# Six-layer local transformer inside a larger block: squares kept in the buffer of the rotated queries and keys, ten places instead of eight for split weight pieces, and the next layer's pieces split at other steps

## The chip, the cores and the metric

The kernel runs on one core of a Trainium2 chip. Its time is the device time of one execution in microseconds (us); lower is better. TensorE is called PE, VectorE DVE, ScalarE ACT, GpSimd POOL, and SyncE, which here issues all transfers, SP.

## The reference

The whole program is two blocks with adaptive layer norm. The first block's second half is a local transformer of six layers over 2 x 1024 tokens of width 128. The change touches only that part. One of its attention layers computes:

```python
qkv = x @ Wqkv                       # x shifted by one token in its upper 64 features
q, k, v = split into 16 heads of 64
q = l2norm(q) * qs
k = l2norm(k) * ksc
q = q * cos * scale + rotate_half(q) * sin * scale
k = k * cos * inv + rotate_half(k) * sin * inv
out = local_attention(q, k, v)       # windows of 32 tokens, each sees itself and the one before
out = out @ Wo
```

`l2norm` divides each head of a token by the root of its sum of squares. After attention and a residual comes a feed-forward part with layer norm and an exact gelu gate, and a second residual. Weights differ from layer to layer.

## The kernel before

`local_transformer` cuts the 2 x 1024 tokens of a layer into 16 slots of 128 tokens, so six layers are 96 slots. One software pipeline runs over all of them: a loop over steps, written out once per engine, in which step i works on several slots at once. In step i, PE projects queries and keys for slot i+2 (`project_qk`, four matrices of 512 columns), turns slot i's rotated queries and keys around (L803), computes slot i's scores (L824), projects the values of slot i+1 (`project_v`, two pieces), weighs the values of slot i-1 (L853) and projects slot i-2 out (L875). Every second step also takes a share of the feed-forward part: `up` and the gates fall into odd steps, `down` into even ones. Each engine works through its own list in the written order, so what stands at a place of the list waits for all that stands ahead of it.

**Weight pieces.** A layer's query, key and value matrix of 3072 columns is cut into six pieces of 512. The kernel multiplies in two parts, so each piece is split: SP loads it into `w_raw` (two buffers in turn, L580), ACT rounds it into `w_high` (L947), and POOL takes the difference into `w_low` (L696). `w_high` and `w_low` have `WS` places, and piece k of the whole run (k = 6 * layer + j) lies in place k % WS. Pieces j = 0 to 3 are queries and keys, 4 and 5 the values. Before a place is filled again, `wait_place` waits for the last matrix product that read it. With eight places, pieces 0 and 1 of a layer find a free place well ahead, while pieces 2 to 5 lie where pieces 0 to 3 of the running layer lie, and can be split only after that layer's last projection from them, in step -3. I write step -k for the step that stands k ahead of the first slot of the next layer, thus step 16 * layer - k. A layer has 16 slots, so step -k is an even step where k is even. There are five such layer boundaries. The first projection from a new query or key piece is in step -2, from a new value piece in step -1.

**When a piece is loaded and split** is set by two tables of step numbers: one in `splits_at`, which ACT and POOL both go by, and one in SP's loop. ACT splits j < 4 in the middle of its step and j >= 4 at the end of it. POOL splits j < 4 between the two halves of a slot's rotation, and j >= 4 one step later: the first of them ahead of the rotation, a second between its halves.

**One slot's norm and rotation.** ACT copies the projections into `qk` (L954) and squares them into `sq` (L960). DVE sums the squares by head (L1076) and takes the larger of that and 1e-24 (L1078, a tiny instruction with two inputs in SBUF). ACT takes logarithm and exponential (L966, L968). DVE scales `qk` by it (L1084, the first instruction of DVE's step), then multiplies with the cosines into `qr` (L1091). POOL multiplies the swapped halves with the sines into `t_sin` (L728, two per half slot) and adds them into `qr` (L733). Every second step POOL also stages the next inputs (L703, L705) and scales the next tables (L715), in odd steps. DVE's residual add (L1131, `h_mid`) and its product for the gate (L1150, `lt_f_gate`) empty banks of PSUM that PE's next products wait for: four banks go round in a ring.

Of the kernel before, what the change touches and what calls it, by code (L numbers as in the profile page):

```python
# [9 lines left out]
ALU = mybir.AluOpType  # L10
ACT = mybir.ActivationFunctionType
AX = mybir.AxisListType

P = 128
# [9 lines left out]
HD = 64  # L24
# [5 lines left out]
INNER = HEADS * HD  # L30
# [361 lines left out]
def local_transformer(nc, A, sb, sem, bank, ident, mean_w, eps, h_in, h_mid, padded):  # L392
# [3 lines left out]
    CHUNKS = ALL // 2  # L396
    BLOCKS = SLOTS // 2
    WCH = 6
    WS = 8
    with ExitStack() as ctx:  # L400
        def buf(name, shape, dt=F32):
            return sb(f"lt_{name}", shape, dt, ctx=ctx)

        w_high = buf("w_high", [P, WS, CH], F32R)
        w_low = buf("w_low", [P, WS, CH], F32R)
        w_raw = buf("w_raw", [P, 2, CH])
# [11 lines left out]
        x_high = buf("x_high", [P, 2, B, BLK], F32R)  # L418
        x_low = buf("x_low", [P, 2, B, BLK], F32R)
        qk = buf("qk", [P, 2, 2 * INNER])  # L420
        sq = buf("sq", [P, 2 * INNER])
        ssq = buf("ssq", [P, 2, 2 * HEADS])
        rn = buf("rn", [P, 2, 2 * HEADS])
        least = buf("least", [P, 2 * HEADS])
        t_sin = buf("t_sin", [P, INNER])
        qr = buf("qr", [P, 2, 2 * INNER])
        q_t = buf("q_t", [P, 2, PAIRS, BLK])
        k_t = buf("k_t", [P, 2, PAIRS, WIN + BLK])
# [25 lines left out]
        S = type("S", (), {n: sem(f"s_lt_{n}") for n in names})  # L454
# [13 lines left out]
        def live(g):  # L468
            return 0 <= g < ALL

        def even(i, back):
            c = (i - back) // 2
            return c if (i - back) % 2 == 0 and 0 <= c < CHUNKS else None
# [11 lines left out]
        def has_look(g):  # L485
            return g % SLOTS >= 2


        def splits_at(i):
            ks = []  # L490
            for layer in range(1, LAYERS):
                for j, at in enumerate((-8, -7, -3, -3, -2, -2)):
                    if i == SLOTS * layer + at:
                        ks.append(WCH * layer + j)
            return ks

        def wait_place(eng, k):

            if k >= WS:
                layer, j = (k - WS) // WCH, (k - WS) % WCH  # L500
                g = SLOTS * layer + SLOTS - 1
# [71 lines left out]
        with nc.Block(no_gpsimd_drain=True) as blk:  # L573
            @blk.sync
            def _(sp):
                def load_w(k):
                    if k >= 2:
                        sp.wait_ge(S.w_low, k - 1)
                    layer, j = k // WCH, k % WCH
                    sp.dma_start(w_raw[:, k % 2, :], A["lt_wqkv"][layer][:, j * CH:(j + 1) * CH]).then_inc(s_w[k % 2], 16)  # L580
# [9 lines left out]
                def load_scale(layer, i):  # L590

                    r = layer % 2
                    if i == 0 and layer >= 2:
                        sp.wait_ge(S.tab_scaled, BLOCKS * (layer - 1))
                    src = A["lt_qkscale"][layer]
                    if i == 0:
                        sp.dma_start(qk_scale[:, r, 0, :], src.to_broadcast([P, 2 * HD])).then_inc(s_scale[r], 16)
                    else:
                        a, h = (i - 1) // 2, (i - 1) % 2
                        to, at = HD * a + 32 * h, HD * a + 32 - 32 * h  # L600
                        sp.dma_start(qk_scale[:, r, 1, to:to + 32], src[:, at:at + 32].to_broadcast([P, 32]))\
                          .then_inc(s_scale[r], 16)

                def load_x(c):
                    if c >= BLOCKS:
                        sp.wait_ge(S.ff_out, c - BLOCKS + 1)
                    if c >= 2:
                        sp.wait_ge(S.staged, c - 1)
                    for f, back in halves:
                        sp.dma_start(x_s[f, c % 2, :, :], block(h_in, c, back, f)).then_inc(s_x[c % 2], 16)  # L610

                def load_v(g):
                    sp.wait_ge(S.v_out, 2 * (g + 1))
                    if g >= 2:
                        sp.wait_ge(S.av, g - 1)
                    if has_look(g):
                        for par in range(2):
                            lo = HD * par
                            sp.dma_start(v[lo:lo + WIN, g % 2, 0, :, :], v[lo + WIN:lo + 2 * WIN, g % 2, WPB - 1, :, :])\
                              .then_inc(S.look, 16)  # L620
                    for par in range(2):
                        lo = HD * par
                        src = v_tok[:, g % 2, par, :].rearrange("p (h d) -> p h d", d=HD)
                        sp.dma_start(v[lo + WIN:lo + 2 * WIN, g % 2, 0, :, :], src[0:WIN]).then_inc(s_v[g % 2], 16)
                        for w in range(1, WPB - 1):
                            sp.dma_start(v[lo:lo + 2 * WIN, g % 2, w, :, :], src[WIN * (w - 1):WIN * (w + 1)])\
                              .then_inc(s_v[g % 2], 16)
                    if has_look(g):
                        sp.wait_ge(S.look, looks(g))
                    for par in range(2):  # L630
                        lo, w = HD * par, WPB - 1
                        src = v_tok[:, g % 2, par, :].rearrange("p (h d) -> p h d", d=HD)
                        sp.dma_start(v[lo:lo + 2 * WIN, g % 2, w, :, :], src[WIN * (w - 1):WIN * (w + 1)])\
                          .then_inc(s_v[g % 2], 16)

                def look_back(g):
                    sp.wait_ge(S.scores, g - 1)
                    sp.dma_start(k_t[:, g % 2, :, 0:WIN], k_t[:, g % 2, :, BLK:BLK + WIN]).then_inc(s_klook[g % 2], 16)

                def load_f_x(c):  # L640
                    sp.wait_ge(S.out_done, 2 * (c + 1))
                    if c >= 1:
                        sp.wait_ge(S.f_mean, c)
                    for f, back in halves:
                        sp.dma_start(f_x[f, :, :], block(h_mid, c, back, f)).then_inc(S.f_x, 16)
# [13 lines left out]
                    load_layer(0, n)  # L659
                for i in STEPS:  # L660
                    for layer in range(1, LAYERS):
                        for j, at in enumerate((-10, -9, -7, -6, -2, -2)):
                            if i == SLOTS * layer + at:
                                load_w(WCH * layer + j)
                    if even(i, -5) is not None and even(i, -5) >= 2:
                        load_x(even(i, -5))
                    if live(i + 1):
                        load_v(i + 1)
                    if live(i + 2) and has_look(i + 2):
                        look_back(i + 2)  # L670
                    if even(i, 3) is not None:
                        load_f_x(even(i, 3))

                    for layer in range(1, LAYERS):
                        n = i - (SLOTS * layer - 11)
                        if 0 <= n < 5:
                            load_scale(layer, n)
                        elif 5 <= n < 9:
                            load_layer(layer, n - 5)
# [13 lines left out]
            def _(pool):  # L693
                def split_low(k):
                    pool.wait_ge(S.w_high, k + 1)
                    pool.tensor_tensor(w_low[:, k % WS, :], w_raw[:, k % 2, :], w_high[:, k % WS, :].bitcast(F32),  # L696
                                       ALU.subtract).then_inc(S.w_low, 1)
# [81 lines left out]
            def _(pe):  # L779
                def project(g, use, k):  # L780
# [4 lines left out]
                    xh, xl = x_high[:, g // 2 % 2, g % 2, :], x_low[:, g // 2 % 2, g % 2, :]  # L785
                    pe.matmul(o, xh, w_high[:, k % WS, :], start=True, stop=False)  # L786
                    pe.matmul(o, xh, w_low[:, k % WS, :], start=False, stop=False)  # L787
# [155 lines left out]
            def _(act):  # L943
# [11 lines left out]

                def square_qk(g):
                    act.wait_ge(S.proj_out, 4 * (g + 1))
                    if g >= 1:
                        act.wait_ge(S.sumsq, g)
                    act.activation(sq[:, :], qk[:, g % 2, :], ACT.Square).then_inc(S.squared, 1)  # L960

                def invert_norms(g):
                    act.wait_ge(S.clamped, g + 1)
# [70 lines left out]
                for i in STEPS:  # L1034
# [8 lines left out]
                    for k in splits_at(i):  # L1043
                        if k % WCH < 4:
                            split_high(k)
# [24 lines left out]
            def _(dve):  # L1070
                def sum_squares(g):
                    dve.wait_ge(S.squared, g + 1)
                    if g >= 2:
                        dve.wait_ge(S.ln, g - 1)
                    q = ssq[:, g % 2, :]
                    dve.tensor_reduce(q, sq[:, :].rearrange("p (h d) -> p h d", d=HD), AX.X, ALU.add).then_inc(S.sumsq, 1)  # L1076
                    dve.wait_ge(S.sumsq, g + 1)
                    dve.tensor_tensor(q, q, least[:, :], ALU.max).then_inc(S.clamped, 1)  # L1078

# [1005 lines left out]
```

## Time and profile before

| what | value |
|---|---|
| median of 3 runs | 2867.06 us |
| lowest, highest | 2858.47, 2876.53 us |
| profiled execution, its own time | 2873.17 us |
| profiled execution, span from first to last instruction | 2871.4 us |
| mean granted PE clock in it | 0.958 |

The profiled execution lies 1.8 us above its own span, and 6 us above the median, inside the spread of the runs. The local transformer is the stretch from about 115 us to about 1830 us of the span. In the profile, "idle before" is the time in which an engine sat still ahead of an instruction, with the instruction that released it. The length of a step is read here from the start of one L1084 on DVE to the start of the next one.

### The profile page before, as it was taken

What the parts mean: (1) busy time and instruction counts of PE and PEld (TensorE: products, weight loads), DVE (VectorE), ACT (ScalarE), POOL (GpSimd) and SP (SyncE); (2) the same over time, 40 slices, a digit from 0 to 9 for tenths busy, and PEclk for the clock granted to TensorE, in tenths of its full rate; (3) what the DMA queues carried; (4) which work ended last, traced back from release to release, by engine and by line L of the source; (5) the groups of instructions that cost most, each with busy time, mean ns of one, the idle gap of its engine ahead of it and who ended that gap; (6) DMA issues with size and microseconds to landing.
All of it is one profiled execution on the core that took longest, in us unless ns stands there. A gap on an engine that the chain in (4) does not pass through costs nothing. (4 is left out here: it accounts for less than half of the span.)

```text
span 2871.4 us, 119349 instructions
## 1 busy us (share of the span) xinstructions
PE 2518.8 (88%) x52916; PEld 2039.6 (71%) x53012; DVE 2187.8 (76%) x2553; ACT 1879.1 (65%) x3665; POOL 1475.6 (51%) x1015
## 2 busy tenths in 40 slices
PE   5469989999999899989999999679999899986998
PEld 2257777777877787777777887457776677765887
DVE  5378888888888888888888887388888888983112
ACT  2357777777777777777777777466666666653443
POOL 0188887788778787877887776011221212211000
PEclk8689999999999999999999999889999999997999
DMA  0223433333343333433342333022232231210000
GB/s 32 60 66 90 99 89 75 84 92 85 76 99 93 82 77 91 98 79 84 89 102 68 79 90 71 16 64 60 46 69 54 52 69 41 63 33 16 15 22 30
DMA packets 274599, 193.97 MB, mean 68 GB/s; under 512 B 117544, under 2 KB 215856, under 8 KB 273968
## 3 DMA queue, kind: packets, MB, share of 16 engines
q1 hardware_dynamic: 274096, 186.49, 27.2%
q8 instruction: 411, 6.73, 1.0%
q14 instruction: 92, 0.75, 0.1%
HBM read 29.10 MB, written 1.05 MB: 10 GB/s over the span
## 5 line engine op out<-in xcount | busy, mean ns | idle before, releaser
L728 POOL TENSOR_TENSOR lt_t_sin<-lt_qk,lt_tab 128x512 f32<-128x512 f32 x384 | 685.3, 1806 | 298.4 <-DVE lt_qk L1084 294.8
L733 POOL TENSOR_TENSOR lt_qr<-lt_qr,lt_t_sin 128x1024 f32<-128x1024 f32 x192 | 454.9, 2369 | 29.3 <-POOL lt_t_sin L728 2.6
L1622 DVE TENSOR_REDUCE fa_neg_max<-bank 128x1 f32<-128x1024 f32 x256 | 301.1, 1217 | 91.1 <-PE bank L1449 90.6
L786 PE MATMUL bank<-lt_w_high,lt_x_high 128*128 128x512 f32 x576 | 283.8, 493 | 71.4 <-POOL lt_w_low L696 50.7
L1562 ACT ACTIVATE fa_prob<-bank,fa_neg_max 128x1024 f32<-128x1024 f32 x128 | 142.5, 1114 | 244.3 <-DVE fa_neg_max L1622 127.6
L1632 DVE STREAM_TRANSPOSE fa_prob_t<-fa_prob 128x1024 f32<-128x1024 f32 x256 | 301.8, 1217 | 0.0
L1472 PE MATMUL bank<-fa_prob_t,fa_v 32*64 32x128 f32 x16384 | 278.8, 276 | 20.0 <-issue 14.7
L1472 PEld LDWEIGHTS bank<-fa_prob_t,fa_v 32*64 32x64 f32 x16384 | 242.9, 131 | 67.1 <-issue 38.7
L1076 DVE TENSOR_REDUCE lt_ssq<-lt_sq 128x32 f32<-128x2048 f32 x96 | 219.1, 2282 | 80.5 <-ACT lt_sq L960 80.2
L803 PE MATMUL bank<-ident,lt_qr 128*128 128x128 f32 x1536 | 234.5, 276 | 32.7 <-POOL lt_qr L733 16.0
L974 ACT COPY lt_v_tok<-bank 128x512 f32<-128x512 f32 x192 | 112.4, 586 | 222.0 <-PE bank L788 222.0
L1380 POOL TENSOR_TENSOR fa_qk_low<-fa_raw,fa_qk_high 128x256 fp32r<-128x256 f32 x128 | 90.0, 729 | 317.3 <-ACT fa_qk_high L1552 317.0
L803 PEld LDWEIGHTS bank<-ident,lt_qr 128*128 128x128 f32 x1536 | 187.1, 142 | 82.4 <-issue 26.6
L954 ACT COPY lt_qk<-bank 128x512 f32<-128x512 f32 x384 | 231.4, 604 | 16.5 <-POOL lt_t_sin L728 4.8
L1084 DVE TENSOR_TENSOR lt_qk<-lt_qk,lt_rn 128x2048 f32<-128x2048 f32 x96 | 228.7, 2382 | 8.9 <-ACT lt_rn L968 8.9
L1091 DVE TENSOR_TENSOR lt_qr<-lt_qk,lt_tab 128x2048 f32<-128x2048 f32 x96 | 230.0, 2396 | 3.3
L787 PE MATMUL bank<-lt_w_low,lt_x_high 128*128 128x512 f32 x576 | 231.6, 402 | 0.7 <-issue 0.7
L788 PE MATMUL bank<-lt_w_high,lt_x_low 128*128 128x512 f32 x576 | 232.1, 403 | 0.0
L875 PEld LDWEIGHTS bank<-lt_prob_t,lt_w_o 128*128 128x128 f32 x1536 | 186.8, 192 | 11.5 <-issue 4.7
L853 PEld LDWEIGHTS bank<-lt_v,lt_prob_t 64*32 64x32 f32 x12288 | 131.2, 107 | 85.1 <-ACT lt_prob_t L995 65.1
L875 PE MATMUL bank<-lt_prob_t,lt_w_o 128*128 128x128 f32 x1536 | 188.3, 275 | 3.6 <-issue 3.6
L853 PE MATMUL bank<-lt_v,lt_prob_t 64*32 64x64 f32 x12288 | 151.6, 229 | 38.8 <-ACT lt_prob_t L995 22.0
(225 smaller groups left out, 5825.7 us busy)
## 6 DMA issues: line engine op xcount, KB each, us to landing
lt_v<-lt_v_tok SPq DMA_DIRECT2D x576, 128.0 KB, 2.4
fa_v<-fa_v_tok SPq DMA_DIRECT2D x256, 128.0 KB
lt_v<-lt_v_tok SPq DMA_DIRECT2D x192, 64.0 KB, 2.1
lt_k_t<-lt_k_t SPq DMA_DIRECT2D x84, 128.0 KB, 2.7
lt_v<-lt_v SPq DMA_DIRECT2D x168, 64.0 KB, 2.0
lt_w_raw<-in_lt_wqkv_dram SPq DMA_DIRECT2D x36, 256.0 KB, 3.9
lt_x_s<-h_in SPq DMA_DIRECT2D x96, 64.0 KB, 2.7
lt_f_x<-h_mid SPq DMA_DIRECT2D x96, 64.0 KB, 2.2
```

The costliest lines, as they stand in the source:

```text
L728: pool.tensor_tensor(dst[:, :, i, :], src[:, :, 1 - i, :], tab[:, g // 2 % 2, 1, at:at + 32].unsqueeze(1).to_broadcast([P, HEADS, 32]), AL ...
L733: pool.tensor_tensor(qr[:, g % 2, half], qr[:, g % 2, half], t_sin[:, :], ALU.add).then_inc(S.rotated, 1)
L786: pe.matmul(o, xh, w_high[:, k % WS, :], start=True, stop=False)
L787: pe.matmul(o, xh, w_low[:, k % WS, :], start=False, stop=False)
L788: return pe.matmul(o, xl, w_high[:, k % WS, :], start=False, stop=True)
L803: mm = pe.transpose(bank[:, turn_bank("turn", g, j), n * P:(n + 1) * P], qr[:, g % 2, (4 * j + n) * P:(4 * j + n + 1) * P], ident[:, :])
L853: mm = pe.matmul(bank[WIN * w:WIN * w + WIN, value_bank(g, par), hp * HD:(hp + 1) * HD], prob_t[f, g % 2, hp, WIN * w:WIN * w + WIN], v[f, ...
L875: mm = pe.matmul(o, w_o[:, layer % 2, hp, :], att_t[:, g % 2, hp, :], start=hp == 0, stop=hp == PAIRS - 1)
L954: act.copy(qk[:, g % 2, j * CH:(j + 1) * CH], bank[:, turn_bank("qk", g, j), :]).then_inc(S.proj_out, 1)
L1472: mm = pe.matmul(bank[d, 4 + a, 0:P].rearrange("p (u r) -> p u r", u=UPQ), v[rows, half % 2, kb, d], prob_t[rows, q % 2, par, :, 32 * kb:3 ...
L1622: dve.tensor_reduce(neg_max[:, u % 2, par:par + 1], bank[:, 2 * par:2 * par + 2, :].rearrange("p a n -> p (a n)"), AX.X, ALU.max, negate=T ...
L1632: dve.transpose(prob_t[:, q % 2, par, u % UPQ, :], prob[:, u % 2, par, :]).then_inc(S.turned, 1)
```

## The change

It does three things: ACT's squares go into the half of `qr` that the same slot's rotated values will take later, and `sq` is gone; with the space, `w_high` and `w_low` get ten places; and both tables of steps are new.

```diff
-    WS = 8
+    WS = 10
...
-        sq = buf("sq", [P, 2 * INNER])
...
         def splits_at(i):
...
-                for j, at in enumerate((-8, -7, -3, -3, -2, -2)):
+                for j, at in enumerate((-10, -8, -6, -4, -3, -2)):
...
-                        for j, at in enumerate((-10, -9, -7, -6, -2, -2)):
+                        for j, at in enumerate((-13, -12, -9, -7, -5, -3)):
                             if i == SLOTS * layer + at:
                                 load_w(WCH * layer + j)
...
                 def square_qk(g):
                     act.wait_ge(S.proj_out, 4 * (g + 1))
-                    if g >= 1:
-                        act.wait_ge(S.sumsq, g)
-                    act.activation(sq[:, :], qk[:, g % 2, :], ACT.Square).then_inc(S.squared, 1)
+                    if g >= 2:
+                        act.wait_ge(S.turned, 4 * (g - 1))
+                    act.activation(qr[:, g % 2, :], qk[:, g % 2, :], ACT.Square).then_inc(S.squared, 1)
...
-                    dve.tensor_reduce(q, sq[:, :].rearrange("p (h d) -> p h d", d=HD), AX.X, ALU.add).then_inc(S.sumsq, 1)
+                    dve.tensor_reduce(q, qr[:, g % 2, :].rearrange("p (h d) -> p h d", d=HD), AX.X, ALU.add).then_inc(S.sumsq, 1)
```

With ten places, pieces 0 to 3 of a layer lie where nothing of the running layer lies, and pieces 4 and 5 lie where pieces 0 and 1 of the running layer lie. The lists of PE and DVE keep their order. On ACT and POOL the splits move.

POOL, steps -2 and -1 at the first boundary, before (L728 and L733 are a half slot's rotation, L696 is a split):

```order
L728 TENSOR_TENSOR lt_t_sin<-lt_qk,lt_tab 128x16x32 x2
L733 TENSOR_TENSOR lt_qr<-lt_qr,lt_t_sin 128x1024
L696 TENSOR_TENSOR lt_w_low<-lt_w_raw,lt_w_high 128x512
L728 TENSOR_TENSOR lt_t_sin<-lt_qk,lt_tab 128x16x32 x2
L733 TENSOR_TENSOR lt_qr<-lt_qr,lt_t_sin 128x1024
L703 CAST lt_x_high<-lt_x_s 128x256
L705 TENSOR_TENSOR lt_x_low<-lt_x_s,lt_x_high 128x256
L696 TENSOR_TENSOR lt_w_low<-lt_w_raw,lt_w_high 128x512
L728 TENSOR_TENSOR lt_t_sin<-lt_qk,lt_tab 128x16x32 x2
```

The same place on POOL in the changed kernel:

```order
L696 TENSOR_TENSOR lt_w_low<-lt_w_raw,lt_w_high 128x512
L728 TENSOR_TENSOR lt_t_sin<-lt_qk,lt_tab 128x16x32 x2
L733 TENSOR_TENSOR lt_qr<-lt_qr,lt_t_sin 128x1024
L728 TENSOR_TENSOR lt_t_sin<-lt_qk,lt_tab 128x16x32 x2
L733 TENSOR_TENSOR lt_qr<-lt_qr,lt_t_sin 128x1024
L696 TENSOR_TENSOR lt_w_low<-lt_w_raw,lt_w_high 128x512
L728 TENSOR_TENSOR lt_t_sin<-lt_qk,lt_tab 128x16x32 x2
L733 TENSOR_TENSOR lt_qr<-lt_qr,lt_t_sin 128x1024
L703 CAST lt_x_high<-lt_x_s 128x256
L705 TENSOR_TENSOR lt_x_low<-lt_x_s,lt_x_high 128x256
L728 TENSOR_TENSOR lt_t_sin<-lt_qk,lt_tab 128x16x32 x2
```

Piece 4's split moves from the head of step -1 to the head of step -2, and piece 5's from the middle of step -1 to its head; no split stands between the halves of step -1's rotation.

POOL in step -6 (as in steps -10 and -4), before:

```order
L728 TENSOR_TENSOR lt_t_sin<-lt_qk,lt_tab 128x16x32 x2
L733 TENSOR_TENSOR lt_qr<-lt_qr,lt_t_sin 128x1024
L728 TENSOR_TENSOR lt_t_sin<-lt_qk,lt_tab 128x16x32 x2
L733 TENSOR_TENSOR lt_qr<-lt_qr,lt_t_sin 128x1024
```

And in the changed kernel:

```order
L728 TENSOR_TENSOR lt_t_sin<-lt_qk,lt_tab 128x16x32 x2
L733 TENSOR_TENSOR lt_qr<-lt_qr,lt_t_sin 128x1024
L696 TENSOR_TENSOR lt_w_low<-lt_w_raw,lt_w_high 128x512
L728 TENSOR_TENSOR lt_t_sin<-lt_qk,lt_tab 128x16x32 x2
L733 TENSOR_TENSOR lt_qr<-lt_qr,lt_t_sin 128x1024
```

An even step that had no split gets one between the halves of its rotation. Step -8 keeps such a split; the odd steps -7 (one split) and -3 (two) lose theirs.

## Rows read from the trace of the kernel before

**Rows 1.** The page, busy time and share of each engine

```profile
PE 2518.8 (88%) x52916; PEld 2039.6 (71%) x53012; DVE 2187.8 (76%) x2553; ACT 1879.1 (65%) x3665; POOL 1475.6 (51%) x1015
```

**Rows 2.** Whom PE waited for, 200 to 1760 us: total, times, longest

```profile
PE bank L786 <- POOL lt_w_low L696: 21.5, 5, 4.6
...
PE bank L786 <- DVE h_mid L1131: 13.7, 23, 1.5
```

**Rows 3.** Windows, one step each: busy by engine, PEclk, DMA share, GB/s

```profile
807.51:823.47 15.96, 15.28 (x333) 12.63 (x333) 13.24 (x14) 11.08 (x22) 11.86 (x6) 1.00 0.34 82
823.47:840.30 16.83, 16.26 (x339) 13.74 (x339) 15.10 (x19) 14.47 (x26) 13.79 (x9) 1.00 0.48 119
478.86:497.19 18.33, 16.30 (x338) 13.64 (x337) 16.95 (x19) 15.16 (x26) 13.76 (x9) 1.00 0.44 104
840.30:857.42 17.12, 15.53 (x335) 13.07 (x335) 14.67 (x14) 11.59 (x23) 13.10 (x7) 1.00 0.34 78
305.45:322.53 17.08, 16.07 (x335) 13.18 (x335) 16.21 (x20) 15.27 (x27) 14.36 (x10) 1.00 0.43 102
371.58:388.68 17.10, 15.74 (x335) 13.19 (x335) 16.34 (x20) 15.85 (x28) 14.38 (x10) 1.00 0.41 96
388.68:406.61 17.93, 15.71 (x335) 12.97 (x335) 14.39 (x16) 11.12 (x21) 15.69 (x8) 1.00 0.36 103
1496.94:1514.41 17.47, 16.28 (x338) 13.39 (x337) 15.02 (x15) 11.34 (x22) 15.74 (x8) 1.00 0.46 125
406.61:428.74 22.13, 17.41 (x336) 14.25 (x336) 17.71 (x19) 15.91 (x28) 18.48 (x12) 0.92 0.32 78
...
1514.41:1537.77 23.36, 17.90 (x333) 14.34 (x333) 17.81 (x20) 15.91 (x28) 18.48 (x12) 0.85 0.27 68
```

**Rows 4.** Timeline of PE at the first boundary's step -1

```profile
419.76 0.47 PE L786 MATMUL bank<-lt_w_high,lt_x_high 128*128 128x512 f32 x1 [4.50 <-POOL lt_w_low L696]
```

**Rows 5.** Timeline of POOL in the last boundary's step -1

```profile
1514.47 3.36 POOL L696 TENSOR_TENSOR lt_w_low<-lt_w_raw,lt_w_high 128x512 fp32r<-128x512 f32 x1 [1.43 <-ACT lt_w_high L947]
...
1526.15 1.27 POOL L696 TENSOR_TENSOR lt_w_low<-lt_w_raw,lt_w_high 128x512 fp32r<-128x512 f32 x1
1527.38 2.51 POOL L728 TENSOR_TENSOR lt_t_sin<-lt_qk,lt_tab 128x512 f32<-128x512 f32 x2
```

**Rows 6.** Timeline of DVE in that step

```profile
1514.41 2.28 DVE L1084 TENSOR_TENSOR lt_qk<-lt_qk,lt_rn 128x2048 f32<-128x2048 f32 x1
1516.72 3.26 DVE L1091 TENSOR_TENSOR lt_qr<-lt_qk,lt_tab 128x2048 f32<-128x2048 f32 x1
...
1528.69 1.24 DVE L1078 TENSOR_TENSOR lt_ssq<-lt_ssq,lt_least 128x32 f32<-128x32 f32 x1
```

**Rows 7.** Timelines of POOL, DVE, PE: an even step with a split between its halves

```profile
853.68 2.37 POOL L733 TENSOR_TENSOR lt_qr<-lt_qr,lt_t_sin 128x1024 f32<-128x1024 f32 x1
...
854.14 1.96 DVE L1078 TENSOR_TENSOR lt_ssq<-lt_ssq,lt_least 128x32 f32<-128x32 f32 x1
...
856.96 0.51 PE L786 MATMUL bank<-lt_w_high,lt_x_high 128*128 128x512 f32 x1 [1.45 <-DVE h_mid L1131]
```

**Rows 8.** Timelines of DVE and POOL: an odd step without a split, 16.83 us long

```profile
825.78 2.29 DVE L1091 TENSOR_TENSOR lt_qr<-lt_qk,lt_tab 128x2048 f32<-128x2048 f32 x1
...
836.80 0.19 DVE L1078 TENSOR_TENSOR lt_ssq<-lt_ssq,lt_least 128x32 f32<-128x32 f32 x1
...
836.93 2.36 POOL L733 TENSOR_TENSOR lt_qr<-lt_qr,lt_t_sin 128x1024 f32<-128x1024 f32 x1
```

**Rows 9.** The same and PE, in an odd step of 18.33 us

```profile
492.41 2.28 DVE L1078 TENSOR_TENSOR lt_ssq<-lt_ssq,lt_least 128x32 f32<-128x32 f32 x1
...
492.31 2.35 POOL L733 TENSOR_TENSOR lt_qr<-lt_qr,lt_t_sin 128x1024 f32<-128x1024 f32 x1
...
495.84 0.63 PE L803 MATMUL bank<-ident,lt_qr 128*128 128x128 f32 x4 [1.48 <-DVE lt_f_gate L1150]
```

**Rows 10.** Groups of ACT, 200 to 1760 us: busy, mean ns, idle before

```profile
L960 ACT ACTIVATE lt_sq<-lt_qk 128x2048 f32<-128x2048 f32 x92 | 176.9, 1923 | 0.0
```

## The prediction

> **What bounds the kernel now.** I begin with the busy shares [rows 1]: PE is busy 88% of the span and DVE 76%, but such shares are averages over parts with different limits. So the next view is time by step inside the local transformer [rows 3]. There are two kinds of undisturbed step. An even one takes 15.96 us, with PE busy for 15.28 of it and its clock fully granted. An odd one takes 16.83 us, again with PE busy nearly all the time. The reader is to see that PE sets the pace there, with little room on POOL and DVE: the odd step at 18.33 us and the even step with one split at 17.12 us have no more PE work, and yet are longer.
>
> The steps around a layer boundary stand out. Step -1 takes 22.13 us at the first boundary and 23.36 at the last, and its mean over the five boundaries is 22.93 (all five lie between 22.1 and 23.7) [rows 3]. The list of waits says why: PE's L786 waited for POOL's `lt_w_low` five times, 21.5 us in all, at most 4.6 [rows 2]. The timeline shows one of them, 4.50 us [rows 4]: it is `project_v`'s second piece, piece 5. POOL splits it only in the middle of step -1, at 1526.15 in the last boundary, after it has split piece 4 at the head of the step and rotated half a slot [rows 5]. The same steps have a granted clock of 0.92 and 0.85 where the others have 1.00 [rows 3]: PE had stood still for those 4.5 us, and part of the work behind it ran at the lower of its two clocks, so the step pays more than the wait.
>
> **Part 1, the squares.** L960 never waited: idle before it is 0.0 us over 92 instructions [rows 10]. So the removed wait for `sumsq` gave no time away. The wait put in its place, for the four turns of slot g-2, is for a value that ACT has already waited for in the same step, when it emptied the fourth of those turns. Nothing queues behind it. DVE's L1076 reads another buffer of the same shape. I price this part at 0; a gain is excluded by the idle of 0.0, and a loss by that earlier wait.
>
> **Part 2, step -1.** Piece 5 is now split at the head of step -1, and no split stands between the halves. ACT finishes `w_high` for it no earlier than it finished piece 4's before, so L696 starts where it does now, just behind the start of DVE's L1084: at 1514.47 against 1514.41 [rows 5, 6]. It takes 3.36 us there instead of 1.27, because it cannot run beside L1084; its tail then holds up L1091, which takes 3.26 us instead of 2.29 [rows 6, 8]. That loss stays. What goes is PE's wait and the low clock. So step -1 becomes the undisturbed odd step plus L1091's delay, 16.83 + (3.26 - 2.29) = 17.8 us. The bounds: 16.8 if that delay is hidden, 19.5 if L1078 collides as described below. I take 17.8, a saving of 22.93 - 17.80 = 5.1 us per boundary. What ends last next is DVE's chain from L1106 over the gate and the norm to the next L1084; the gate's products on PE will no longer be late.
>
> **Part 3, an even step with a split.** This is what the change pays with. Steps -10, -6 and -4 get a split between the halves of their rotation, as step -8 has today. That step shows the price [rows 7]. POOL's second half is later by one split, and its L733 runs from 853.68 to 856.05. DVE's tiny L1078, ready at 854.14, sits 1.96 us until L733 is over. L1131 follows it, and PE waits 1.45 us for the bank that L1131 empties. The step takes 17.12 us against 15.96 [rows 3], so a split costs 1.16 us, nearly its whole duration of 1.27 us [rows 5], although neither ACT nor POOL is the bound by its share. Bounds: 0, if POOL's idle time took it up, and 1.27. I take 1.16, which is this very case. Three new ones cost 3.5 us per boundary.
>
> The Trainium skill, page "SBUF — State Buffer", section "SBUF: two separate sides", states this rule: a DVE instruction with two SBUF inputs and a GpSimd instruction that reads SBUF exclude each other over one port pair, and whichever begins first holds it to its end. The trace agrees (L1078 takes 1.96 us in one place and 0.19 in another) [rows 7, 8]. By that rule alone each of the three splits would cost its full 1.27 us, and the sum would be 0.3 us per boundary worse.
>
> **Part 4, the odd steps that lose splits.** Step -7 took 17.08 us with its split, against 16.83 [rows 3]: 0.25 saved. Step -3 took 17.10 with two splits: 0.27 saved. Together 0.5 us per boundary; the bounds are 0 and, should both steps have been long ones without their splits (part 7), a loss of 2.5.
>
> **Part 5, step -2.** It took 17.93 and 17.47 us at the first and last boundary, 17.91 in the mean of five (17.1 to 19.5) [rows 3]. It will have one split at its head, which delays the rotation as an even split does, 15.96 + 1.16, and one ACT copy instead of two at its end and one new at its beginning, for which I add 0.3, half of L947's 0.6 us or so. That is 17.4 us, 0.5 saved. Bounds: 16.9, if split and copy overlap, and 18.4, if two delays add as in the worst of the five before.
>
> **Part 6, SP.** The loads are spread: each piece is asked for a step or more ahead of its split, and each waits for a split that stands at least one step earlier. No load follows a split of the same step. The kernel before leaves its loads of pieces 4 and 5 less room than that, and its step -1 waits for POOL's order and not for a load. So I price it at 0; the bounds are 0 and, should the load of piece 5 come late, the whole of part 2.
>
> **The sum.** Per boundary 5.1 (part 2) - 3.5 (part 3) + 0.5 (part 4) + 0.5 (part 5) = 2.6 us; five boundaries, 13 us.
>
> **Part 7, collisions in odd steps.** Odd steps without a split come in two lengths. In the short one, L1078 begins at 836.80, just ahead of L733 at 836.93, and takes 0.19 us [rows 8]. In the long one L733 begins at 492.31 and L1078, 0.10 us behind, takes 2.28 us; then L1150 is late and PE waits 1.48 us [rows 9]. The step grows from 16.83 to 18.33, by 1.5 us [rows 3], on a difference of 0.23 us. I count ten such long steps: seven among the 15 in the three odd steps behind the boundaries, and three of the five steps -9. An even step with a split ahead leaves PE early against DVE (PE waited for L1131), which is the favourable side, and step -9 will now follow one. That saves 4.5 us, which I count in full; for the 15 steps behind the boundaries I have no reason either way and leave them as they are. The bounds are a gain of 15 us (all ten gone) and a loss of 12 (the other eight of those 15 long as well). The sum is then 13 + 4.5 = 17.5, some 18 us.
>
> The profiled execution's own 2873.2 us becomes 2855. It stood 6 us above the median of 2867.06, so against the median I forecast 2849 us, 0.6% faster.
>
> **Rivals.**
> - *Splits in even steps are hidden.* If PE is the bound in even steps, and late DVE work is caught up in the next step, the three splits cost near 0 at all boundaries. That is 17.5 us more: saving about 35 us, 2832 us. For it speaks PE's busy 15.28 of 15.96 us; against it step -8, which took 17.1 us at each of the five boundaries. Chance 0.15.
> - *L1078 collides in step -1.* Reading on from the last boundary: without the split, L728's second pair would start at 1526.15 and run 2.51 us [rows 5], so L733 would start at about 1528.75; L1078 starts at 1528.69 [rows 6]. A margin of 0.06 us decides. If it loses, each boundary gives back 1.7 us, 8.5 in all: saving about 9, 2858 us. Chance 0.25.
> - *Slower: every odd step behind an even split collides.* The mechanism is that of part 7, in steps -9, -7, -5 and -3. If DVE's chain reaches L1078 more than 0.13 us later in the step than now, L733 is ahead in all of them. Twenty steps at 1.5 us are 30, of which 4.5 are there today; with the collision in step -1 that is 34 us against the sum of 13: 21 us slower, 2888 us. For it speaks that seven of 15 odd steps behind the boundary do just this; against it that PE is early after such a step. Chance 0.06.
> - *The change doesn't do what it says.* Piece 5 still comes late, by its load or by ACT, and PE waits on. Then parts 3 and 4 alone count: (3.5 - 0.5) x 5 = 15 us slower, 2882 us. Against it: on both lists piece 5 now stands where piece 4 stood, and piece 4 was in time. Chance 0.03.
>
> The forecast itself has 0.51.
>
> **How the numbers follow.** The range is to leave out no more than 2 in 10. At the low end it takes in most of the first rival; at the high end the collision in step -1 with part 7 gone against me, and the 4 or 5 us by which medians of three runs wander (the three runs span 18 us). That gives 2828 to 2868. A measurement of this kernel can tell about 1% from no change, that is 29 us. Faster than 2838.4 needs most of the first rival: 0.16. Slower than 2895.7 needs the third one in full and more: 0.02. The rest, 0.82, is within 1%.
>
> **What the profile of the changed kernel would show.** The wait of L786 for `lt_w_low` after 200 us gone, and the granted clock 1.00 in step -1: part 2 right. Step -1 at 17.8 with L1078 at 0.2 to 1.3 us, or at 19.5 with L1078 at 2.3 and L733 just ahead of it: the first or the second case. Steps -10, -8, -6, -4 at 17.1 and PE's waits for `h_mid` up from 23 to some 35 times: part 3 right; the same steps at 16.0 would prove it wrong. Steps -9 to -3 at 16.8 or at 18.3: part 7. The forecast is wrong if PE waits in step -1 for something I don't see, since the five steps -1 carry 25 us, more than any other part.

## The result and the profile after

The changed kernel takes 2851.15 us in the median of six runs (2844.54 to 2851.74), the kernel before 2868.32 us (six runs, 2858.47 to 2876.53). The ratio is 0.9934 with a 95% interval of 0.9914 to 0.9955: 17 us by the medians, 0.66%, forecast 18. The profiled executions lie farther apart, 2871.4 to 2847.8 us of span, because that of before stood above its median and that of after a little below. Of those 23.6 us, 21 lie in steps 5 to 84, which hold all five boundaries. These two rows of windows give that stretch before and after (length, busy time by engine, granted PE clock, DMA share, GB/s):

```profile
238.20:1618.91 1380.71, 1279.70 (x26722) 1070.81 (x26801) 1189.18 (x1281) 1048.29 (x1871) 1094.20 (x641) 0.99 0.36 87
```

```profile
237.15:1596.80 1359.65, 1275.20 (x26802) 1063.65 (x26801) 1186.69 (x1282) 1039.86 (x1871) 1084.26 (x641) 1.00 0.37 88
```

PE's busy time fell by 4.5 us, with the clock at 1.00 where it was 0.99; the other 16.5 us are idle time of PE. Next, whom PE waited for from 200 to 1760 us in the changed kernel (total, times, longest), beside [rows 2]:

```profile
PE bank L786 <- DVE h_mid L1131: 24.3, 28, 1.8
PE bank L853 <- ACT lt_prob_t L995: 22.2, 44, 0.5
PE bank L853 <- issue: 16.1, 23, 1.8
PE bank L824 <- issue: 14.6, 13, 2.5
PE bank L803 <- DVE lt_f_gate L1150: 3.8, 7, 0.9
```

The wait of 21.5 us for `lt_w_low` has gone altogether. The wait for `h_mid` has grown from 13.7 us in 23 times to 24.3 in 28, and that for `lt_f_gate` is small. Both are read step by step in these windows of the changed kernel, beside [rows 3]. They are step -10 (796.12) and two more even steps with a split, step -1 of the first and the third boundary, and steps -2 and -1 of the last:

```profile
796.12:813.21 17.09, 15.88 (x335) 12.90 (x334) 14.38 (x14) 11.59 (x23) 13.07 (x7) 1.00 0.31 70
829.91:847.01 17.10, 16.15 (x340) 13.55 (x339) 14.10 (x16) 11.82 (x23) 13.07 (x7) 1.00 0.33 76
898.36:915.44 17.08, 15.73 (x334) 12.92 (x334) 14.66 (x14) 11.59 (x23) 13.06 (x8) 1.00 0.32 75
949.84:967.72 17.88, 15.64 (x334) 12.91 (x333) 16.88 (x20) 15.31 (x27) 17.30 (x11) 1.00 0.38 93
...
407.02:424.26 17.24, 16.73 (x344) 14.10 (x342) 16.55 (x19) 14.97 (x27) 16.81 (x10) 1.00 0.40 101
1495.62:1515.49 19.87, 17.67 (x334) 13.97 (x333) 17.08 (x20) 15.43 (x27) 17.26 (x11) 0.91 0.38 95
1475.46:1495.62 20.16, 17.21 (x335) 14.16 (x334) 13.89 (x14) 11.69 (x23) 14.60 (x7) 0.92 0.30 77
```

Step -1 fell from 22.13 us to 17.24 at the first boundary, with the clock now at 1.00; four of the five take 17.1 to 17.9 us. The even steps with a split take 17.1 us each, all 20 of them between 17.08 and 17.39. The collision in POOL's and DVE's lists is there as in [rows 7]. In an even step of the changed kernel (timelines of POOL and DVE):

```profile
843.26 2.37 POOL L733 TENSOR_TENSOR lt_qr<-lt_qr,lt_t_sin 128x1024 f32<-128x1024 f32 x1
```

```profile
844.31 1.37 DVE L1078 TENSOR_TENSOR lt_ssq<-lt_ssq,lt_least 128x32 f32<-128x32 f32 x1
```

L1078 is ready at 844.31 and ends with L733, which is done at 845.63. In step -1, though, the close race that was one of the rivals is won. At the first boundary (POOL, then DVE):

```profile
407.08 3.36 POOL L696 TENSOR_TENSOR lt_w_low<-lt_w_raw,lt_w_high 128x512 fp32r<-128x512 f32 x1 [1.80 <-ACT lt_w_high L947]
...
421.44 2.37 POOL L733 TENSOR_TENSOR lt_qr<-lt_qr,lt_t_sin 128x1024 f32<-128x1024 f32 x1
```

```profile
409.33 3.26 DVE L1091 TENSOR_TENSOR lt_qr<-lt_qk,lt_tab 128x2048 f32<-128x2048 f32 x1
...
421.33 0.19 DVE L1078 TENSOR_TENSOR lt_ssq<-lt_ssq,lt_least 128x32 f32<-128x32 f32 x1
```

L696 again runs 3.36 us beside L1084 and holds up L1091 to 3.26 us, as forecast. L1078 begins 0.11 us ahead of L733 and takes 0.19 us. It is so at all five boundaries (0.10 to 0.13 us ahead). Where PE has no standstill of its own in step -1, at the first, second and fourth boundary, the step takes 17.25, 17.09 and 17.12 us. The 17.88 and 19.87 us of the third and fifth hold standstills of PE of 1.65 and 1.82 us, for which the profile shows no cause ("issue"; last section).

Here is the account by steps, the mean over the five boundaries, each step read from one first DVE instruction to the next:

| step | before | after | change x 5 | forecast x 5 |
|---|---|---|---|---|
| -1 | 22.93 | 17.84 | -25.5 | -25.5 |
| -2 | 17.91 | 17.85 | -0.3 | -2.5 |
| -10, -6, -4 | 16.34, 16.49, 16.04 | 17.21, 17.10, 17.09 | +12.7 | +17.5 |
| -7, -3 | 17.30, 17.16 | 17.14, 17.01 | -1.5 | -2.5 |
| -9 | 17.72 | 17.40 | -1.6 | -4.5 |
| all others of steps 5 to 84 | | | -4.9 | 0 |

### The profile page after: what moved, and what is told of

The parts are those of the page before. It is cut to its first block and busy times, and to the rows that moved or that the text cites. A ratio compares the mean times of both kernels' runs of the same rounds, so it can differ in the third digit from the quotient of the medians.

```text
span 2847.8 us, 119442 instructions
## 1 busy us (share of the span) xinstructions
PE 2514.4 (88%) x53012; PEld 2031.5 (71%) x53012; DVE 2183.9 (77%) x2553; ACT 1872.0 (66%) x3665; POOL 1468.1 (52%) x1015
## 5 line engine op out<-in xcount | busy, mean ns | idle before, releaser
L728 POOL TENSOR_TENSOR lt_t_sin<-lt_qk,lt_tab 128x512 f32<-128x512 f32 x384 | 686.2, 1809 | 279.3 <-DVE lt_qk L1084 276.8
L733 POOL TENSOR_TENSOR lt_qr<-lt_qr,lt_t_sin 128x1024 f32<-128x1024 f32 x192 | 455.2, 2371 | 28.4 <-POOL lt_t_sin L728 1.3
L1076 DVE TENSOR_REDUCE lt_ssq<-lt_qr 128x32 f32<-128x2048 f32 x96 | 219.1, 2282 | 77.9 <-ACT lt_qr L960 77.7
L803 PE MATMUL bank<-ident,lt_qr 128*128 128x128 f32 x1536 | 233.2, 275 | 22.2 <-POOL lt_qr L733 14.7
L803 PEld LDWEIGHTS bank<-ident,lt_qr 128*128 128x128 f32 x1536 | 186.6, 141 | 70.5 <-issue 18.9
L1084 DVE TENSOR_TENSOR lt_qk<-lt_qk,lt_rn 128x2048 f32<-128x2048 f32 x96 | 225.2, 2346 | 13.4 <-ACT lt_rn L968 13.4
L1091 DVE TENSOR_TENSOR lt_qr<-lt_qk,lt_tab 128x2048 f32<-128x2048 f32 x96 | 231.6, 2412 | 3.3
```

The source lines that it names most:

```text
L728: pool.tensor_tensor(dst[:, :, i, :], src[:, :, 1 - i, :], tab[:, g // 2 % 2, 1, at:at + 32].unsqueeze(1).to_broadcast([P, HEADS, 32]), AL ...
L733: pool.tensor_tensor(qr[:, g % 2, half], qr[:, g % 2, half], t_sin[:, :], ALU.add).then_inc(S.rotated, 1)
L803: mm = pe.transpose(bank[:, turn_bank("turn", g, j), n * P:(n + 1) * P], qr[:, g % 2, (4 * j + n) * P:(4 * j + n + 1) * P], ident[:, :])
L1091: dve.tensor_tensor(qr[:, g % 2, :].rearrange("p (a h d) -> p a h d", a=2, h=HEADS), qk[:, g % 2, :].rearrange("p (a h d) -> p a h d", a=2 ...
```

## The experiments

All ratios are against the kernel before on the same chip, with their 95% intervals. The changed kernel's is 0.9934 [0.9914, 0.9955]. Step lengths are those of the one profiled execution of each kernel.

**The squares alone.**

```diff
+ ACT squares into qr[:, g % 2, :], waits for S.turned; sq is gone; DVE sums qr
  WS = 8, both tables of steps as before
```

> The kernel before with the squares alone moved into qr; eight places and both old tables stay. My theory: this part is worth nothing, because ACT never waited ahead of L960; so 2868 us within 3 either way, and steps -1 still near 22.9 us. Rival: freeing the one buffer of squares lets ACT run ahead and is part of the gain; then 2860 us or less.

The ratio is 1.0009 [0.9988, 1.0029]. Steps -1 took 22.79 us in the mean, and PE waited 22.8 us for `lt_w_low` in five times. This part is worth nothing by itself; it only makes room for the two places.

**One number put back.**

```diff
-                for j, at in enumerate((-10, -8, -6, -4, -3, -2)):
+                for j, at in enumerate((-10, -8, -6, -4, -2, -2)):
```

> The changed kernel with one number put back: piece 4 is split in step -2 with piece 5, as before the change, so that POOL again does piece 4 at the head of step -1 and piece 5 between the halves of its rotation. Pieces 0 to 3, ten places, squares in qr and the loads stay as changed. My theory: the wait in step -1 comes from this order alone; it returns with 4.5 us at each boundary and the lower clock behind it, step -1 goes from 17.8 back to some 22.9 us, step -2 loses its split (17.85 to 16.7 or so), together 5 x (5.1 - 1.1) = 20 us slower than the changed kernel, so no faster than the kernel before (ratio 0.9934 + 0.007 = 1.000). Rival: the wait came from ACT's or SP's side, or from the lack of places; then it stays away and the time is that of the changed kernel, 0.9934.

The ratio is 1.0002 [0.9986, 1.0019], 0.7% above the changed kernel: the whole gain went with one number. Step -1 came back to 22.97 us in the mean and step -2 fell to 16.57. Windows of step -1 at the first and last boundary:

```profile
407.78:429.83 22.05, 17.37 (x337) 14.19 (x336) 17.72 (x19) 15.92 (x28) 18.50 (x12) 0.92 0.33 81
1514.35:1537.97 23.62, 18.45 (x334) 14.48 (x333) 17.84 (x19) 15.93 (x28) 18.49 (x12) 0.86 0.29 74
```

The wait and the low clock are both there again, although places and loads are those of the changed kernel. The one number moves piece 4's copy on ACT as well as its split on POOL. But ACT had both copies done by 408.29, and POOL came to piece 5 only at 419.53, without having waited for anything there (timelines of ACT and POOL):

```profile
407.16 1.13 ACT L947 CAST lt_w_high<-lt_w_raw 128x512 fp32r<-128x512 f32 x2
...
419.53 1.26 POOL L696 TENSOR_TENSOR lt_w_low<-lt_w_raw,lt_w_high 128x512 fp32r<-128x512 f32 x1
```

So the wait came from POOL's order. The run also shows what pieces 0 to 3 ahead are worth: against the kernel before, this one has three more even steps with a split and no gain. The reverse, pieces 4 and 5 moved alone and pieces 0 to 3 left where they were, was not run.

**Odd steps in place of even ones.**

```diff
-                for j, at in enumerate((-10, -8, -6, -4, -3, -2)):
+                for j, at in enumerate((-11, -9, -7, -5, -3, -2)):
...
-                        for j, at in enumerate((-13, -12, -9, -7, -5, -3)):
+                        for j, at in enumerate((-14, -13, -10, -8, -6, -4)):
```

> The changed kernel with pieces 0 to 3 split in the odd steps -11, -9, -7 and -5 in place of the even ones -10, -8, -6 and -4, loads to match. My theory: a split costs 1.1 us in an even step, where L1078 then sits behind L733, and some 0.3 us in an odd one. So the four even steps fall from 17.1 to 16.0 us, the odd ones rise from 16.6 to about 17.0, and the time is 2851 - 5 x 4 x 0.8 = about 2835 us. Rival: a split costs its own length wherever it stands, since POOL's time is what counts; then 2851 us.

The ratio is 0.9894 [0.9854, 0.9934], 0.4% below the changed kernel, but with intervals that overlap, so the difference is not clear of noise: about 11 us where 16 were expected. In the profiled executions steps 5 to 84 differ by 7.3 us (1352.4 against 1359.7). Windows, an odd step with its split and the even step behind it:

```profile
842.87:859.94 17.07, 15.79 (x335) 13.15 (x334) 16.21 (x19) 15.26 (x27) 14.34 (x10) 1.00 0.36 86
859.94:876.34 16.40, 15.98 (x339) 13.48 (x338) 13.96 (x15) 11.17 (x22) 14.67 (x7) 1.00 0.40 93
```

The odd step takes 17.1 us, which is 0.3 more than the 16.83 of [rows 3] and 0.5 more than the 16.6 of a short odd step in the changed kernel. The even step behind it takes 16.4 and not 16.0. So a split in an odd step costs some 0.7 to 0.9 us and not 0.3, one in an even step 1.1.

**L1078 taken out**, from the changed kernel and from the kernel before. The floor of 1e-24 is added to the sum of squares inside the logarithm, in place of a maximum; for any sum that isn't vanishingly small this is the same number.

```diff
-                    dve.wait_ge(S.sumsq, g + 1)
-                    dve.tensor_tensor(q, q, least[:, :], ALU.max).then_inc(S.clamped, 1)
...
-                    act.wait_ge(S.clamped, g + 1)
+                    act.wait_ge(S.sumsq, g + 1)
...
-                    act.activation(rn[:, g % 2, :], ssq[:, g % 2, :], ACT.Ln).then_inc(S.ln, 1)
+                    act.activation(rn[:, g % 2, :], ssq[:, g % 2, :], ACT.Ln, bias=least[:, 0:1]).then_inc(S.ln, 1)
...
+                act.wait_ge(S.cleared, 4)
```

> The changed kernel without L1078: the floor of 1e-24 is added inside ACT's logarithm (as its bias) in place of DVE's maximum. My theory: the price of a split in an even step and the long odd steps both come from L1078 sitting behind POOL's L733. With it gone, even steps with a split fall from 17.1 to 16.2 us or less (20 of them, 18 us or more), long odd steps vanish (about nine at 1.5 us, 13 us), and L1078's own 0.2 us leaves the chain of each step: 2851 - 35 = about 2815 us. Rival: POOL's sheer amount of work sets an even step with a split; then these stay at 17.1, only the odd ones gain, 2838 us.

> The kernel before without L1078, its floor as the bias of ACT's logarithm. My theory: ten long odd steps (15 us), step -8 (1 us each, 5 us) and the shares of steps -7, -3 and -2 (about 5 us) go, PE's wait of 4.5 us for piece 5 stays: 2868 - 25 = about 2843 us, so that the change is worth more on this base than on its own (28 us against 17). Rival: the long steps have another cause; then 2860 us or more.

The ratios are 0.9819 [0.9782, 0.9857] and 0.9887 [0.9850, 0.9925]. Without L1078 the changed kernel is 1.2% faster, some 33 us by the ratios where 36 were expected, and the kernel before 1.1%, some 32 us where 25 were expected. Windows of the changed kernel without L1078, an even step with a split and the odd step behind it:

```profile
820.58:835.62 15.04, 14.95 (x333) 12.55 (x332) 12.64 (x14) 11.58 (x23) 12.39 (x7) 1.00 0.29 64
835.62:852.88 17.26, 16.06 (x335) 13.21 (x335) 15.92 (x18) 14.86 (x27) 14.49 (x10) 1.00 0.46 110
```

Even steps with a split fell from 17.1 to 15.39 us in the mean, which is what even steps without one take there: the price of a split in an even step was L1078's collision, and is gone with it. But part of it comes back: the odd steps -9 to -3 rose from 17.04 to 17.59 us; what sets them then was not looked into. The expectation for the kernel before was too small. It missed that the ordinary even step pays for L1078 too. In the kernel before, an even step without a split (DVE, then POOL):

```profile
821.55 0.59 DVE L1078 TENSOR_TENSOR lt_ssq<-lt_ssq,lt_least 128x32 f32<-128x32 f32 x1
```

```profile
819.74 2.36 POOL L733 TENSOR_TENSOR lt_qr<-lt_qr,lt_t_sin 128x1024 f32<-128x1024 f32 x1
```

L1078 waits here as well, until L733 ends at 822.10. Without it the even steps of steps 5 to 84 take 36.5 us less together and the odd ones 5.3 us more. By the ratios the change is worth the same 0.7% on this base as on its own, and not more.

**The split done twice**, with L1078 and without it.

```diff
                 def split_low(k):
                     pool.wait_ge(S.w_high, k + 1)
+                    if k >= WCH and k % WCH < 4:
+                        pool.tensor_tensor(w_low[:, k % WS, :], w_raw[:, k % 2, :], w_high[:, k % WS, :].bitcast(F32),
+                                           ALU.subtract).then_inc(S.spare, 1)
+                        pool.wait_ge(S.spare, 4 * (k // WCH - 1) + k % WCH + 1)
```

> The changed kernel with POOL's split of pieces 0 to 3 done twice (the same subtraction into the same place, 20 more instructions of 1.28 us); ACT and the loads unchanged. My theory: POOL's order is what an even step with a split waits for, by way of L1078 behind L733. So steps -10, -8, -6 and -4 go from 17.1 to 18.4 us, 20 x 1.28 = 25 us, 0.9% slower than the changed kernel. Rival: ACT's copy L947 is what costs the 1.1 us and POOL has room; then these steps stay at 17.1.

> The same double split, in the kernel without L1078 (floor as the bias of ACT's logarithm). My theory: DVE no longer meets L733 in its small instruction, so the 20 extra splits cost little: 0 to 8 us against the kernel without L1078 alone. Rival: once POOL's list is longer, L1084 or L1091 meets POOL's instructions in its place, or the turn of qr on PE waits for L733; then 20 us or more, as with L1078.

The first ratio is 0.9934 [0.9910, 0.9958], equal to the changed kernel's within some 7 us either way, so 25 us of work on POOL cost little or nothing. My theory fell, and so did the rival: 18 of the 20 even steps neither rose to 18.4 us nor stayed at 17.1, but fell to between 15.9 and 16.0. The other two did take 18.4. Windows of an even step with the double split and of the odd step behind it:

```profile
866.68:882.60 15.92, 15.79 (x339) 13.51 (x339) 12.95 (x16) 11.82 (x23) 12.91 (x8) 1.00 0.31 69
882.60:900.42 17.82, 16.26 (x338) 13.56 (x338) 16.65 (x20) 14.58 (x26) 15.21 (x10) 1.00 0.51 130
```

The timelines say why (L737, L1082 and L807 are L733, L1078 and L803 in this kernel; DVE, POOL, PE):

```profile
881.04 0.24 DVE L1082 TENSOR_TENSOR lt_ssq<-lt_ssq,lt_least 128x32 f32<-128x32 f32 x1
```

```profile
881.66 2.37 POOL L737 TENSOR_TENSOR lt_qr<-lt_qr,lt_t_sin 128x1024 f32<-128x1024 f32 x1 [0.43 <-POOL lt_t_sin L732]
```

```profile
884.09 0.66 PE L807 MATMUL bank<-ident,lt_qr 128*128 128x128 f32 x4 [0.99 <-POOL lt_qr L737]
```

Two splits push L733 so far back that L1078, ready at 881.04, is done before it starts. In the two steps of 18.4 us L1082 came 0.05 and 0.27 us behind L737 instead and took 2.36 and 2.13 us. The other even steps run at full pace, and the delay shows up in the next one. PE waits 0.99 us for L733's half of `qr`, DVE's next L1084 meets POOL (3.59 us instead of 2.28 in this place), and the odd steps -9 to -3 take 17.86 us in the mean instead of 17.04. With one split or two, the pair of steps shown takes 33.7 us, against 32.8 without any [rows 3]. Without L1078 the double split has nothing to dodge. The ratio is 0.9883 [0.9858, 0.9908] against 0.9819, 0.65% or some 18 us for 25 us of work, with PE waiting 16.7 us in 17 times for L733 where it was 2.6 us. Here the rival came nearer than my theory.

**All six pieces in mid-step, none in steps -2 and -1**, with L1078 and without.

```diff
-                for j, at in enumerate((-10, -8, -6, -4, -3, -2)):
+                for j, at in enumerate((-11, -9, -7, -5, -3, -3)):
...
+ loads at (-14, -13, -10, -8, -6, -4)
+ ACT and POOL split all six where they split j < 4 before
```

> The changed kernel with pieces 0 to 3 split in steps -11, -9, -7 and -5, and pieces 4 and 5 both in the middle of step -3, on ACT and POOL alike, so that steps -2 and -1 hold no split. Theory: step -1 loses L1091's delay behind a split that starts with L1084, 17.8 to 16.8, and step -2 falls to some 16.9, 5 x 1.5 us = 7 us less than the odd-step kernel (ratio to the kernel before 0.9894), so some 0.987. Rival: POOL carries two splits out of step -3, its L715 meets L1084 as before the change, and step -2 stays at 17.5 or more; then no gain over the odd-step kernel.

> The mid-step kernel without L1078. If where the splits stand mattered only through L1078, this equals the changed kernel without L1078 (ratio 0.982) within 3 us; if steps -2 and -1 still pay for the splits at their heads there, it is 5 us or so faster, ratio 0.980.

The ratios are 0.9891 [0.9862, 0.9919] and 0.9774 [0.9737, 0.9810]. With L1078 it gains nothing over the odd-step kernel: step -1 takes 17.04 us, step -2 17.95, the rival's outcome. Without L1078 step -2 is 16.35 us, step -1 17.33, and this is the fastest kernel of the study, 2812.6 us in the median against 2874.7 for the kernel before on the same chip, 2.3%. Its ratio is lower than that of the changed kernel without L1078 by 0.45% (0.9774 against 0.9819), with intervals that overlap, so the 5 us that I expected of the splits at the heads of steps -2 and -1 is neither shown nor refuted. In the profiled executions steps -2 are shorter by 8.3 us in all, and 8.3 us lie in the three of them in which the other kernel has a standstill of 2.4 to 2.5 us (last section). Its windows of steps -2 and -1 at the third boundary:

```profile
915.43:931.84 16.41, 15.09 (x332) 12.52 (x332) 13.92 (x14) 11.26 (x22) 15.43 (x8) 1.00 0.35 90
931.84:948.95 17.11, 15.62 (x334) 13.21 (x335) 14.93 (x19) 14.79 (x27) 14.02 (x10) 1.00 0.37 89
```

## Why the prediction was right, point by point

- **Size and sign.** Forecast 0.6% faster, measured 0.66%. Its core is the balance of a gain of 25 us in five steps and a price of 13 us in fifteen others, and both parts were found where they were forecast. That the sum came out so near is partly luck. The price was 4.8 us smaller than forecast, parts 4, 5 and 7 together gave 6.1 us less, and 4.9 us came from steps that the forecast left at 0.
- **Part 1, the squares, 0.** Shown: 1.0009 with the squares alone, and ACT's idle time before the squares is still 0.0 us in that run.
- **Part 2, step -1, 17.8 us.** Measured 17.84 in the mean. The cause, the order on POOL, is shown by the kernel with one number put back. The agreement to 0.04 us is luck. Where PE doesn't stand still for its own reasons, step -1 takes 17.1 to 17.25 us: L1091 is held up to 3.26 us at each boundary as forecast, but 17.1 is only some 0.5 us above the 16.6 of a short odd step, so about half of that delay is hidden. Two standstills that the forecast didn't have lift the mean to 17.84.
- **Part 3, +1.16 us for each new even step with a split.** Each such step took 17.1 us as forecast; that L1078 behind L733 is the cause is shown by the kernel without L1078. PE's waits for `h_mid` went from 23 to 28 times and not to some 35. The term was 17.5 us and measured 12.7, since steps -10 and -6 had not been at 15.96 us before but at 16.34 and 16.49. Step -6 stood behind step -7's split, and I had left that out; what lengthened step -10 was not looked into. The odd-step kernel shows the same 0.4 us behind each odd split. But what I said of the cause, that a split costs nearly its own length, holds for one split only. The double split shows that the price is that of meeting L1078 and doesn't grow with POOL's work as long as L1078 is dodged; the doubled work has a price of its own, 18 us, once L1078 is gone. The rule of the shared port pair that I cited from the Trainium skill ("SBUF — State Buffer", "SBUF: two separate sides") gives how long a collision lasts, and L1078's 1.37 us above agree with it. It does not say what a longer list costs, and my sentence that by it each split would cost its full length doesn't follow from it. By that reading the double split would have been 25 us slower, and it was not slower within the noise.
- **Part 4, 2.5 us.** Measured 1.5.
- **Part 5, step -2, 17.4 us.** Measured 17.85, but no single step says so. The two without a standstill of over 1 us in the scores' products (L824) take 16.97 and 16.93 us; the other three take 17.28, 17.89 and 20.16, with standstills of 1.27, 1.94 and 2.54. The 0.3 us that I added for ACT's copies was not there. With the split at its head taken away it is 16.57.
- **Part 7, 4.5 us in step -9.** It gave 1.6 us there: two of the five steps -9 are still long. Only one of them collides (18.35 us, L1078 2.35). In the other (18.81 us) L1078 takes 0.19 us, and PE had a standstill of 1.83. Elsewhere long odd steps became fewer. Of the odd steps from 5 to 84 other than step -1, 11 took over 18 us before and 7 after. Outside steps -9, -7 and -3 it was 7 before and 3 after, four times 1.5 us, which the table's last line holds. This is not shown to be the change's doing: the kernel with one number put back has the changed kernel's splits in steps -10 to -4 and still 6 of them. That an even split would leave the next odd step short was right three times in five in step -9.
- **Rivals.** Hidden splits: no, 17.1 us each. The collision in step -1: no, by 0.10 to 0.13 us where I had read 0.06. The slower case did not come: of 20 odd steps -9 to -3 four were long.

## What to carry to other kernels

A stall at the end of a chain of prefetches may need only its last pieces split earlier. Here one number carried the whole gain, though it was not run alone. Moving the others "well ahead" put them into steps with less room, and gave half of the gain back. Before moving work on an engine that looks half idle, read which tiny instruction of another engine stands beside it: here one of 0.2 us with two operands in SBUF decided some 30 us, and folding it into an activation's bias was worth twice the whole change. And where the cost comes from two lists meeting, test the slope with doubled work, since the first unit may cost much and the second little.

## What the runs showed of the hardware that I had not expected

PE sometimes stands still for 1 to 2.5 us in the middle of a run of small matrix products, with nothing in the profile that it waits for ("issue"), and after some of these the clock falls. The last boundary's step -2 in the changed kernel is the worst case. PE's timeline there:

```profile
1480.31 1.09 PE L824 MATMUL bank<-lt_k_t,lt_q_t 64*32 64x64 f32 x87
1483.93 0.66 PE L824 MATMUL bank<-lt_k_t,lt_q_t 64*32 64x64 f32 x41 [2.54 <-issue]
...
1485.32 2.53 PE L906 MATMUL bank<-lt_f_gate,lt_w 128*128 128x256 f32 x6
```

After 2.54 us of standstill the six products of L906 take 2.53 us, where they take 1.46 at full clock. The windows of PE's products just ahead of them and of those six give the granted clock:

```profile
1484.60:1485.32 0.72, 0.72 (x4) 0.59 (x5) 0.59 (x1) 0.00 (x0) 0.72 (x1) 1.00 0.08 23
1485.32:1487.85 2.53, 2.53 (x8) 1.93 (x7) 0.79 (x2) 0.59 (x1) 2.45 (x3) 0.55 0.00 0
```

The step's mean clock is 0.92. Together with 1.82 us in the next step, after which the clock falls too, this makes two steps of 20 us where 17 are usual. The length of the standstill alone does not decide: the clock stayed at 1.00 in the changed kernel behind standstills of 1.94 us (step -2) and 1.65 us (step -1) at the third boundary and 1.83 us in a step -9. The kernel before has one such step -2 (19.52 us, a standstill of 1.87), the squares-only kernel two (20.08 us with 2.28, and 19.57), the odd-step kernel two (19.92 us with 2.54, and 19.21), the mid-step kernel one (19.84 us), the double split without L1078 one (19.64 us), the changed kernel without L1078 two (19.79 us with 2.49, and 19.99). The kernel with one number put back has none (17.10 us at most, with 1.68). Of the standstills of over 1 us in steps 5 to 84 of all eleven kernels, 30 of 82 fall on step -2, and the kernel before without L1078 has none there. What feeds them was not tried and stays open.
